# Expert outputs placed by adding indirect DMAs in place of store, gather, gate and add

## What is computed

```python
h = _layernorm(x, axis=-1) * (1 + cb) + sb
# _L0_ffn_ref: each token has one expert in the end, the highest numbered of its top two
for i in range(n_exp):
    wi = wf[:, i:i + 1]
    h = relu(xf * wi @ w1[i] + b1[i])
    y = h @ w2[i] + b2[i]
    out = where(wi > 0, y, out)
x = x + gb * out
```

## Time and profile before

| what | us |
|---|---|
| median of 3 runs | 853.75 (853.61 to 856.53) |
| the profiled execution, its own time | 855.83 |
| its span | 854.1 |
| busy in it: TensorE, VectorE, GpSimd, ScalarE | 810.3, 603.8, 637.8, 396.6 |
| span up to the last pair's scores | about 762 |
| the 30 expert tiles | about 762 to 837 |
| behind the last tile | about 837 to 854.1 |

### The profile page before, as it was taken

One profiled execution on the slowest core, in us unless ns is written; L12 is line 12 of the kernel. 1 busy time (PEld: TensorE's weight loads), 2 busy tenths in 40 slices (PEclk: granted clock), 3 DMA queues, 4 the chain that ended last, 5 costly groups with the idle time before them and its releaser, 6 DMA issues.

```text
span 854.1 us, 15058 instructions
## 1 busy us (share of the span) xinstructions
PE 810.3 (95%) x5236; PEld 484.3 (57%) x5236; DVE 603.8 (71%) x1143; ACT 396.6 (46%) x645; POOL 637.8 (75%) x325
## 2 busy tenths in 40 slices
PE   4878999999999999999999999999999999999991
PEld 2535555565655555555555555555555554458891
DVE  8897777777778777778787878787878665355023
ACT  3654444444444444444444445444444444345550
POOL 3488998989899797979797989898978775311233
PEclk8979999999999999999999999999999999999996
DMA  9000010101010101001010101010101012335772
GB/s 261 28 1 13 14 26 13 28 14 26 13 27 13 27 14 20 21 8 32 7 33 2 39 1 39 2 38 3 26 1 26 2 27 76 86 100 160 203 218 84
DMA packets 84521, 37.87 MB, mean 44 GB/s; under 512 B 56928, under 2 KB 72672, under 8 KB 84384
## 3 DMA queue, kind: packets, MB, share of 16 engines
q1 hardware_dynamic: 83424, 34.82, 16.9%
q0 software_dynamic: 1024, 2.10, 0.8%
HBM read 30.48 MB, written 6.15 MB: 43 GB/s over the span
## 4 chain that ended last, share of the span: by engine, by line
PE 93%; DVE 4%; POOL 1%; issue 1%; DMA 1%; ACT 1%; POOLq 0%; DVEq 0%
PE ps_o L480 28%; PE ps_m L443 9%; PE ps_x L431 9%; PE ps_s L464 7%; PE ps_s L466 7%; PE ps_s L470 7%; PE ps_s L468 7%; PE ps_s L531 4%; PE ps_s L668 3%; PE ps_s L677 3%; PE ps_s L489 2%; DVE mx L1204 1%; PE ps_m L498 1%; PE ps_s L680 1%; PE ps_s L443 1%
## 5 line engine op out<-in xcount | busy, mean ns | idle before, releaser
L1028 POOL TENSOR_TENSOR big<-big,probs 128x1024 f32<-128x1024 f32 x180 | 440.3, 2446 | 70.0 <-ACT probs L777 49.9
L1204 DVE TENSOR_REDUCE mx<-ps_m 128x2 f32<-128x1024 f32 x240 | 294.0, 1225 | 109.7 <-PE ps_m L443 109.2
L777 ACT ACTIVATE probs<-ps_s 128x1024 f32<-128x1024 f32 x256 | 249.0, 1024 | 170.5 <-PE ps_s L470 170.4
L480 PE MATMUL ps_o<-probs,c_all 128*64 128x512 f32 x1024 | 248.0, 605 | 0.0
L480 PEld LDWEIGHTS ps_o<-probs,c_all 128*64 128x64 f32 x1024 | 62.1, 136 | 97.2 <-ACT probs L777 41.1
L443 PE MATMUL ps_m<-k_hi,q_hi 64*128 64x512 f32 x480 | 108.4, 444 | 2.2 <-DVE mx L1204 2.2
L464 PE MATMUL ps_s<-q_hi,k_hi 64*128 64x512 f32 x512 | 102.2, 394 | 0.0
L470 PE MATMUL ps_s<-neg_row,one_row 64*128 64x512 f32 x512 | 102.0, 390 | 0.0
L466 PE MATMUL ps_s<-q_hi,k_lo 64*128 64x512 f32 x512 | 101.7, 391 | 0.0
L468 PE MATMUL ps_s<-q_lo,k_hi 64*128 64x512 f32 x512 | 101.7, 390 | 0.0
L443 PEld LDWEIGHTS ps_m<-k_hi,q_hi 64*128 64x128 f32 x480 | 46.8, 184 | 87.2 <-issue 76.9
(11 more groups left out here) (295 smaller groups left out, 986.8 us busy)
## 6 DMA issues: line engine op xcount, KB each, us to landing
big<-in_experts SPq DMA_DIRECT2D x30, 322.0 KB, 3.5
big<-rd_dram SPq DMA_DIRECT2D x60, 128.0 KB
big<-in_wqk SPq DMA_DIRECT2D x16, 256.0 KB, 2.7
neg_row<-nm SPq DMA_DIRECT2D x256, 0.5 KB, 2.0
big<-in_expert_w SPq DMA_DIRECT2D x8, 256.0 KB, 4.1
xs_dram<-zero SPq DMA_DIRECT2D x2, 960.0 KB, 7.3
moe<-xs_dram SPq DMA_DIRECT2D x10, 192.0 KB, 3.6
ys_dram<-moe SPq DMA_DIRECT2D x10, 192.0 KB, 3.7
```

The source lines that it names most:

```text
L480: ins = nc.tensor.matmul(ps_o[64 * h:64 * h + 64, :], c_all[:, (p // HP) * TB + kt, :], probs[:, st % 4, h, :], start=(kt == 0), stop=(kt ...
L777: nc.scalar.activation(probs[:, st % 4, :, :], ps_s[:, 2 * (st % 2):2 * (st % 2) + 2, :], ACT.Exp, scale=SCALE).then_inc(s["probs"], 1)
L1028: V.tensor_tensor(acc[:, buf(p, half), :, :], first, probs[:, st % 4, :, :], ALU.add).then_inc(s["added"], 1)
L1204: V.reduce_max(mx[:, :, kh, qt], max_banks(q, n), AX.X).then_inc(s["max_reduced"], 1)
```

## The change

The result lives in DRAM (`out`) from early on. When a batch's attention is done, `base(b)` stores `x_sb` of that batch there (512 KB). Each token row in `xs_dram` is 130 words long instead of 128 (`ROW`), and the last two hold the token's number. The scatter takes them along, so a slot that is loaded tells to which row of `out` its output belongs. The numbers of empty slots are written beforehand by 30 small DMAs (`spare_rows`), each naming a row of its own behind the result, in 1920 spare rows that `out` has now and that are not returned.

Each tile's output is multiplied by the gate in SBUF, by GpSimd for tiles 0 to 6 (`scale`) and by VectorE from tile 7 on (`T_DVE`). It is then added into `out` by one indirect DMA with `compute_op=ALU.add` (`place`). The stores to `ys_dram`, the gathers, the last multiplications, the last additions and the five stores are gone. Outputs have 14 buffers (`NY`), each with a semaphore of its own. TensorE's bias matmuls are left for tiles 0 to 6 only. Its order of tiles is one loop, in which only tile 15 has its transpose behind down_e(14).

```diff
+NY = 14
+ROW = D + 2
...
-                                           w2_all[:, expert[k], c * P:(c + 1) * P], start=(c == 0), stop=(c == 3 and k >= NA * GS))
-                if k < NA * GS:
+                                           w2_all[:, expert[k], c * P:(c + 1) * P], start=(c == 0), stop=(c == 3 and k >= T_DVE))
+                if k < T_DVE:
                     ins = nc.tensor.matmul(ps_s[:, 3, 0:D], ones_sq[0:1, :], b2_sb[i][0:1, :], start=False, stop=True)
...
+            for k in range(NG * GS):
+                up_e(k % (2 * GS), k)
+                if k == T_LOG:
+                    logits(1)
+                if k + 1 < NG * GS and k + 1 != NA * GS:
+                    slots_T((k + 1) % (2 * GS), k + 1)
+                if k and k != NA * GS:
+                    down_e((k - 1) % (2 * GS), k - 1)
+                if k == NA * GS - 1:
+                    down_e(k % (2 * GS), k)
+                    slots_T((k + 1) % (2 * GS), k + 1)
...
+            def token_ids(g):
+
+                pool.wait_ge(group_in[g % 2], 16 * (g // 2 + 1))
+                V.tensor_copy(token[:, GS * g:GS * g + GS],
+                              xs_row[:, g % 2, :, D].bitcast(I32)).then_inc(s["token_ids"], 1)
+
+            def place(k):
...
+                nc.gpsimd.indirect_dma_start(out=out, out_offset=bass.IndirectOffsetOnAxis(ap=token[:, k:k + 1], axis=0),
+                                             in_=ys[k % NY], in_offset=None,
+                                             compute_op=ALU.add).then_inc(placed[k % NY], 16)
+
+            def scale(k):
+
+                pool.wait_ge(s["y_copied"], k + 1)
+                V.tensor_tensor(ys[k], ys[k], mod[:, 0, 5, :], ALU.mult).then_inc(s["y_scaled"], 1)
+
             scatter(0)
             inverse_root(0)
+            token_ids(0)
+            token_ids(1)
             inverse_root(1)
-            scatter(1)
...
+            pool.wait_ge(base_out[0], 16)
+            for k in range(NG * GS):
+                if k == T_SCAT:
+                    scatter(1)
+                    token_ids(4)
+                if k == NA * GS:
+                    pool.wait_ge(base_out[1], 16)
+                if k < T_DVE:
+                    scale(k)
+                place(k)
+                if k in (1, 4):
+                    token_ids(k // GS + 2)
...
+                ge(dve, placed[k % NY], 16 * (k // NY))
+                y = ys[k % NY]
+                V.tensor_tensor(y, ps_s[:, 3, 0:D], b2_sb[i], ALU.add).then_inc(s["y_copied"], 1)
+                dve.wait_ge(s["y_copied"], k + 1)
+                V.tensor_tensor(y, y, mod[:, k // (NA * GS), 5, :], ALU.mult).then_inc(s["y_scaled_1"], 1)
...
+                if 1 <= p <= NSL // 2 + 1:
+                    for n in range(2 * p - 2, min(2 * p, NSL)):
+                        spare_rows(n)
+                if p == HP + 1:
+                    base(0)
...
-                if g >= 2:
-                    store(g - 2, par)
+                if g == 1:
+                    base(1)
...
-            sp.wait_ge(result_out, 16 * len(PARTS))
+            for n in range(NY):
+                sp.wait_ge(placed[n], 16 * ((NG * GS - 1 - n) // NY + 1))
+            for b in range(B):
+                sp.wait_ge(base_out[b], 16)
```

More of the change, by code:

```diff
@@ L166, in build @@
         slot = sb("slot", [P, NT], I32)
+        token = sb("token", [P, B * NSL], I32)
+        spare = sb("spare", [P, NSL, ROW - D], I32)
         eid = sb("eid", [P, B * NSL], I32)
@@ L252, in build @@
             "y_product": "a tile's outputs (tensor)",
-            "y_copied": "and in SBUF (scalar, then vector with b2)",
-            "done": "a part of the result (vector)",
+            "y_copied": "and in SBUF (scalar, from tile T_DVE on vector with b2)",
+            "y_scaled": "times the gate, the first tiles (gpsimd)",
+            "y_scaled_1": "from tile T_DVE on (vector)",
+            "token_ids": "the tokens of a group's slots, batch 0 (gpsimd)",
+            "token_ids_1": "batch 1 (vector)",
         }
@@ L268, in build @@
         expert_in = [sem(f"expert_in{n}") for n in range(2 * GS)]
-        group_out = [sem(f"group_out{n}") for n in range(2)]
-        gathered = [sem(f"gathered{g}") for g in range(len(PARTS))]
-        result_out = sem("result_out")
+        placed = [sem(f"placed{n}") for n in range(NY)]
+        base_out = [sem(f"base_out{b}") for b in range(B)]
         block = ctx.enter_context(nc.Block())
@@ L653, in slots_T @@
                 ge(pe, s["slots_in"], k)
[L654 removed]
+                nc.tensor.transpose(ps_s[:, 2, 0:P], xs_row[:, g % 2, i % GS, 0:D], ident[:]).then_inc(s["slots_T"], 1)
             expert = {}
@@ L1454, in y_out, with token_ids @@
                 dve.wait_ge(s["y_product"], k + 1)
[L1455 to L1468, removed]
-            y_out(2 * GS - 1, NG * GS - 1)
[L1471 to L1476, removed]
+                ge(dve, placed[k % NY], 16 * (k // NY))
[3 more added lines that the diff above has]
+                V.tensor_tensor(y, y, mod[:, k // (NA * GS), 5, :], ALU.mult).then_inc(s["y_scaled_1"], 1)
+            def token_ids(g):
+                dve.wait_ge(group_in[g % 2], 16 * (g // 2 + 1))
+                V.tensor_copy(token[:, GS * g:GS * g + GS],
+                              xs_row[:, g % 2, :, D].bitcast(I32)).then_inc(s["token_ids_1"], 1)
+            for k in range(T_DVE, NA * GS):
+                y_out(k % (2 * GS), k)
+            slots_out(GS, NA * GS)
+            for k in range(NA * GS, NG * GS):
+                if k < NG * GS - 1:
+                    slots_out((k + 1) % (2 * GS), k + 1)
+                if k % GS == 0:
+                    token_ids(k // GS)
+                if k > NA * GS:
+                    y_out((k - 1) % (2 * GS), k - 1)
+            y_out(2 * GS - 1, NG * GS - 1)
         @block.sync
```

104 lines of the change are left out of this document (48 added, 56 removed).

## The result

The median is 849.28 us (849.0 to 849.56, 4 runs), against 854.75 (853.61 to 856.53, 4 runs) for the kernel before: the ratio is 0.9934, 95% interval 0.9913 to 0.9955, so the gain is small and clear of noise. The forecast was 839.8 with a range of 836.0 to 850.0. Direction and range held, and 8.4 us of the gain of 13.9 did not come. The profiled execution took 849.1 us, with a span of 847.3, so it can be read against the 840.2 of the forecast's sum: 7.1 us are to be found. (By the medians it is 9.5, since the profile that the forecast started from lay 2.1 above its median and this one does not.)

A forecast was written before the change was run, and what follows sets the result against it. TensorE's list and waits, then a serial 17.44 us tail, were taken to bound the kernel. Tail 11.7 plus TensorE 2.2 gave 13.9 us off the 853.75 median: 839.8 us, range 836.0 to 850.0.

The forecast's parts named there:

- the forecast's sum: Whole kernel: 11.7 us from the tail plus 2.2 from TensorE, 13.9 off the span of 854.1, giving 840.2.
- GpSimd keeping up: GpSimd's indirect DMAs: at 1.26 us each, 24 places from about 797.2 catch up by about tile 20.
- rival (B): GpSimd at the end: adding makes the instruction dearer and GpSimd sets the pace; 844 to 853 us, 17%.
- the landing: Last adding DMA, from its instruction's start until it lands: 4.5 us, bounds 2.4 and 6.5.
- scatter and gather cost the same 0.95: GpSimd's instruction price: argument against a dearer adding DMA, since scatter and gather address different sides at equal cost.
- faster: Whole kernel: chance, given as 79%, of a gain beyond the 0.5% (4.3 us) that a measurement can tell.
- The tail: Behind tile 29's output: 17.44 us replaced by 5.7 (gate, DMA start, landing, end), so 11.7 less (9.7 to 13.8).
- The second scatter: GpSimd behind six places: still starts at 786.26, covered by 0.6 us, unless a place costs over 1.9.
- TensorE's list: TensorE's tiles: bias gone from tiles 7 to 14 and new order at tile 15, 2.2 us gained (0.8 to 4.1).
- What was to cost nothing: VectorE's gate in batch 1 (0.33 a tile), SyncE's 30 small DMAs (1.5 us) and group loads: all hidden.
- (C): Transfers behind the second scatter: adds don't overlap, 3.5 us each, median about 881; 17% for slower.
- (D): Expert loads under the adds stall TensorE by 11 to 14 us, cancelling the gain: 849 to 858, about 6%.

The follow-up runs named there:

- e5: Changed kernel with the places of tiles 6 to 14 as plain scatters without addition (their tokens lose x): 846.4 us, ratio 0.9875.
- e1: Changed kernel with all places as plain scatters without addition, so the residual is left out: 840.0 us, ratio 0.9824.
- e2: Changed kernel with the second scatter one place earlier (T_SCAT = 5), whole result kept: 851.34 us, ratio 0.9947.
- v1_carry: Changed kernel, but batch 1's slot rows carry x, VectorE adds the gated output, and GpSimd places it plainly; whole result: 844.27 us, ratio 0.9853.
- e4: Changed kernel with 512-byte rows, no spare-row DMAs, and outputs added to spare rows, so the result keeps only x: 849.13 us, ratio 0.9923.
- e3: Changed kernel with all places plain and the second scatter one place earlier (T_SCAT = 5); residual left out: 842.11 us, ratio 0.9835.
- v2_late: v1_carry with a group's three loads of x issued behind the weights of all its three experts: 844.44 us, ratio 0.989.
- v1_carry_5: v1_carry with the second scatter one place earlier (T_SCAT = 5): 844.85 us, ratio 0.9868.
- v2_late_5: v2_late with the second scatter one place earlier (T_SCAT = 5): 844.75 us, ratio 0.9881.

## Why the prediction was right and wrong, step by step

**The step that failed** is "one indirect DMA costs it 1.26 us (0.96 busy and 0.30 of issue)", in the part on GpSimd keeping up. An adding DMA costs 1.86. The mechanism was named as rival (B), with its threshold: over (835.5 - 797.2) / 23 = 1.66 us a place, GpSimd paces the end. The measured price lies 0.20 above it, 4.6 us over 23 places, and the queue began at 798.81 in place of 797.2, 1.6 more: 835.5 + 6.2 = 841.7, which is the last place's start. With 1.0 for the landing that is the missing 7.1 us. e5 shows it by taking the price away for nine places and leaving TensorE's stall, e1 by taking it away wholly, with which the stall went too, and e2 by giving TensorE time that the end did not use. By itself the cheaper queue is worth little: 1.8 us in e5 (0.90 in place of 2.66), since right below it lies TensorE's late tile 29, the second cost, for which the sum had nothing. Only both together give the 7.2 of e1. I gave prices from 1.8 to 2.25 a chance of 17%; "scatter and gather cost the same 0.95" was no evidence for an instruction that also adds. That the range held was width: at 1.86 and with nothing else changed, rival (B) gives 797.2 + 23 x 1.86 = 840.0 for the last start, 4.5 late, and 844.3 for the time, 5 below the measured one. Two slips in that working change nothing here: its 1.73 us a place delay the last start by 1.5 (837.0 against 835.5), not 1.7, and the shares that it adds up for "faster" come to 81, not 79.

In the same place the prediction weighed a rule of the Trainium skill, "Collectives: The Full Stack", section "The bandwidth ceiling: the fold count and why AG ≠ RS ≠ AR": an adding DMA, which the page describes in a reduction between cores, emits two source descriptors for each piece. By it, as an estimate, the instruction was to be busy for 1.43 us; the rows say 1.554. So the rows agree with its direction, and the estimate made from it was 0.12 short. They don't show descriptors.

**The tail.** The 17.44 us are gone. The gate took 0.32 with its handover (838.71 to 839.03), as forecast, and the handover 0.76 to 0.78 wherever GpSimd had caught up. The landing was taken as 4.5 from the instruction's start, and its median over 30 is 4.4. But the last one ends with the span 5.6 behind its start, 1.0 more than the 4.6 of the sum. Plain places end 5.0 to 5.1 behind, adding ones 5.6 in all four kernels, and the 0.6 between them is as much as the instruction is longer. So the addition costs the transfer nothing that can be seen here, and what was mis-sized is the plain landing at the end, for which "a plain scatter needs 3.0" was the wrong row.

**The second scatter.** "If the place costs more than 1.9, the scatter moves": with gate and handovers a tile costs GpSimd about 2.9 against TensorE's 2.51, and the cover of 0.6 us was used up. The scatter moved by 1.31. The forecast's 1.9 for a tile had the handover between gate and place at 0.2 (1.9 - 0.45 - 1.26), and it is 0.76 to 0.78: with a plain place a tile costs about 2.2 (0.45 + 0.78 + 1.01 in e1), so the cover was thinner than 0.6 from the start.

**TensorE's list.** The bias went as forecast: up_e(8) to up_e(14) is 785.74 to 797.69, 1.99 a tile where 2.06 was taken, and down_e(14) started at 800.28 (800.35 forecast). Then up_e(15) came at 804.22 and not at 802.5. The group's load was issued 2.0 later than before (800.19 against 798.20), 1.3 by the scatter and 0.7 since it came 3.73 behind the last scatter's start, not 3.0; up_e(15) lost 1.7 of these 2.0. From up_e(15) to up_e(17) passed 6.37 us and not 3.8: the low clock, 2.6, for which the sum had nothing. Tile 29 was in SBUF 4.2 late (838.71, not 834.5). In the changed kernel this cost nothing, since GpSimd was later still. In v1_carry, where GpSimd waits for tile 29, it is what is left.

**What was to cost nothing.** It held: VectorE never waited for an output buffer, SyncE's 30 small DMAs and the longer rows cost no time in this kernel (e4, with the reserve made there), and TensorE's steps in batch 1 are 2.01 (up_e(17) to up_e(27), 810.59 to 830.69), although the DMA engines are 91% busy. Rivals (C) and (D) did not occur: adds start every 1.86 and land at most 6.1 behind their start, so they overlap.

**Left open.** From the last scatter's start to the issue of the group's load it takes 2.4 us in e1 to e3, 3.4 to 3.7 in the changed kernel, e4 and e5, 2.5 in v1_carry, 4.3 in v2_late, and 2.7 in v1_carry_5 and v2_late_5. It isn't the rows' length (e4), and plain places behind the scatter don't cure it (e5). In all the long ones the scatter follows an adding place without a break, and where GpSimd stood idle for 2.0 to 2.4 us between the two (e2, v1_carry_5, v2_late_5) it is 2.4 to 2.7. But v1_carry has no break either, at 2.5, and the kernel before has 3.0 with no place at all. No run tried this apart, and the cause isn't settled, nor is why the span ends 5.0 us behind a last plain place whose kind lands in 3.7 at the median (e1).

## What to carry to other kernels

An addition in an indirect DMA is paid on the engine that issues it, here 0.6 us each, and no run here shows a cost in the transfer. Where such instructions queue up behind a block that can't be moved, count the queue from the block's end: (time left) / (number) is the price at which they begin to set the end, and no gain upstream shows until it is undercut. Then look for what lies right below: here the cheap queue alone gave back 1.8 us, and with the stall gone as well it was 7.2. Price an operation that no row shows by its upper bound in such a queue, or keep half of it plain, as v1_carry does by doing the addition on an engine with room.

## What the runs showed of the hardware

An indirect DMA of 128 rows of 512 bytes keeps GpSimd busy for 1.554 us with `compute_op` add and 0.968 without. After a wait of TensorE in this stage the granted clock fell to about its lower level for one to three groups of matmuls, and up_e took 2.04 to 2.08 us in place of 0.89 to 1.16. It did so behind waits for slots of 1.92 (changed kernel), 1.02 (e4), 1.15 (e5), 0.58 (v1_carry), 1.75 (v2_late) and 1.89 (v2_late_5), and did not behind those of 0.95 and 1.35 (v1_carry_5), so the length of that wait alone doesn't decide it. Nor does the list: at up_e(4) it fell in v1_carry_5 and not in v1_carry, where TensorE had the same list up to there and was busy for 4.91 of the 6.00 us ahead in both (764 to 770 and 767 to 773).
